# A graph layer with a mixture of experts: the gating moves from the last stage into the FFN stage

## The chip, the cores and the metric

The kernel runs on one core of a Trainium2 chip, as one launch. The metric is the device time of a launch in microseconds. A core has TensorE (PE), VectorE (DVE), ScalarE (ACT), GpSimd (POOL) and SyncE (SP), each with a queue of its own that runs in order, and 16 DMA engines that all queues share. Engines wait for each other through semaphores.

## What is computed

There are 6250 nodes of 256 features and 206,250 edges. A graph attention layer comes first; it is the same in both kernels. Then each node's row is normalised (this row is called y below), two of 16 experts are chosen for it, and their outputs, weighted by the two gates, are added to y. The sum is normalised again, scaled, shifted, and added to the node's row (x_all below).

```python
x = x + _L0_gnn_ref(_layernorm(x), edge_index, W, a_src, a_dst, gamma, beta)   # graph attention
x = x + _L0_ffn_ref(_layernorm(x)[None], gate_w, gate_b, w1, b1, w2, b2, fgamma, fbeta)[0]
...
def _L0_ffn_ref(x, gate_w, gate_b, w1, b1, w2, b2, gamma, beta):
    gate_logits = x @ gate_w + gate_b
    topk_vals, topk_idx = jax.lax.top_k(gate_logits, K)
    topk_w = jax.nn.softmax(topk_vals, axis=-1)
    h = jax.nn.relu(jnp.einsum('bsh,ehf->bsef', x, w1) + b1)
    expert_out = jnp.einsum('bsef,efh->bseh', h, w2) + b2
    sel = jnp.take_along_axis(expert_out, topk_idx[:, :, :, None], axis=2)
    moe = jnp.sum(topk_w[..., None] * sel, axis=2)
    y = x + moe
    mu = jnp.mean(y, axis=-1, keepdims=True)
    var = jnp.var(y, axis=-1, keepdims=True)
    return (y - mu) / jnp.sqrt(var + EPS) * gamma + beta
```

Everything is float32. The two gates of a node sum to 1.

## The kernel before

The 6250 nodes are 49 tiles of 128 (the last has 106). The stages run one after the other, and each ends when all its engines are done.

The graph stage (stage3) runs over the tiles. GpSimd gathers rows of source nodes with indirect DMAs, and the other engines weigh and sum them. Between this work the finishing of earlier tiles is woven in (class Finish): the inner and the outer normalisation, the choice of experts, and the lists of nodes per expert. For each tile SyncE writes y to y_rows in DRAM (keep, L1746 to L1749) and, once the tile's lists are ready, the 16 pieces of the lists (record, L1751 to L1757). ScalarE writes y of a tile into one buffer (L1708) and waits first until the last tile's y has been sent from it.

The last two tiles are finished in last_tiles. SyncE's queue holds the write of y of tile 46, the load of the first FFN bias b1T (L1789, in which each element of the transposed bias is an element of the load), and the writes of y of tiles 47 and 48. GpSimd's queue holds the loads of the first quarter of the expert weights, four iotas (L197 to L203), and six list scatters (L1673), two for each of tiles 46, 47 and 48. VectorE chooses the experts of each tile (choose, settle), which gives the scatters their places.

The list stage (stage5) makes from the lists, with a gather and a chain of small VectorE operations, the tables put_all (twice the node, plus 0 for its first choice and 1 for its second), get_all (the node) and the expert of each FFN tile.

The FFN stage (stage6) runs over some 105 tiles of 128 (node, choice) pairs, sorted by expert. It is a pipeline of steps, four to a pass of a loop. In step i TensorE transposes tile i's rows (L2090), does the first product of tile i-1 (L2099, with w1_t, a copy of the expert's weights that VectorE makes at L2132) and the second product of tile i-3 (L2108). VectorE in step i copies the weights of tile i, waits for tile i's predecessor to be transposed and writes the indices of the fetch of tile i+3 (get_at, L2124), waits for a delivery to have landed and writes the indices of the delivery of tile i-3 (put_at, L2140), waits for the second product and adds the second bias b2 (L2143, into o_sb). ScalarE copies the transposed rows (L2056), applies bias and relu (L2062), and issues the load of b2. GpSimd in step i issues the fetch of tile i+3 (L2014, a gather of rows of y_rows into xt), then the delivery of tile i-3 (L2023, a scatter of rows of o_sb into chosen). A delivery waits until the one before it has landed. SyncE loads the other quarters of the weights.

The last stage (stage7) runs over 7 groups of 7 tiles. SyncE loads both chosen rows of each node (back, L2313 to L2319) into two buffers. VectorE makes diagonal matrices of the gates (diag, L2258), ScalarE makes y again from x_all (L2204), and TensorE sums both rows, weighted, and y in PSUM (L2247 to L2249). VectorE takes the statistics of the sums (L2266 to L2271) and the scale (L2277, L2278), ScalarE normalises (L2212), and VectorE makes three passes over 7 tiles at once: times gamma (L2285), plus beta (L2286), plus x_all (L2287). GpSimd issues the outputs (L2335, L2338). In VectorE's queue group g's scale comes ahead of the sums of group g+1, and the passes of group g behind them.

## Time and profile before

| | us |
|---|---|
| median of 3 runs | 2841.47 (2836.97 to 2843.8) |
| the profiled execution, its own time | 2831.7 |
| its span in the trace | 2830.0 |

| stretch of the span, us | what runs |
|---|---|
| 0 to 2224 | the first stages and the graph stage |
| 2224 to 2264 | the last two tiles |
| 2264 to 2276 | the list stage |
| 2276 to 2700 | the FFN stage |
| 2700 to 2830 | the last stage |

Busy over the whole span: TensorE 1787.1 us (63%), VectorE 1656.7 (59%), ScalarE 1154.7 (41%), GpSimd 1839.1 (65%). Times are in microseconds from the span's start. In a timeline a row gives start, duration, engine, line, operation, what it writes and reads, and in brackets how long the engine had been idle and what released it. SPq and ACTq are DMAs issued by SyncE and ScalarE. A row with a count (x2) runs from the first start to the last end. In groups by line "busy" is the sum, then the mean of one in ns, then the idle time ahead of them with what ended it; "issue" is idle time in which nothing that the profile shows was waited for.

### The profile page before, as it was taken

To read this page: it belongs to the slowest core of one execution; us is meant where nothing else is said; L and a number is where in the kernel's file an instruction comes from. 1 tells how busy PE (TensorE), PEld (TensorE's weight loads), DVE (VectorE), ACT (ScalarE), POOL (GpSimd) and SP (SyncE) were. 2 spreads that over 40 slices of the span, in tenths; PEclk is the share of its full clock that TensorE was granted. 3 is DMA by queue.
4 is the path that set the end of the run, shared out by engine and by line. 5 is a ranking of instruction groups with operands and counts; after the bars stand their busy time and mean duration, and the time that the engine had idled before them with its cause. 6 is when DMAs were issued, how large, how long until landed. Compare 5 with 4: busy or idle time off the path is not lost. (4 is left out here: it accounts for less than half of the span.)

```text
span 2830.0 us, 43516 instructions
## 1 busy us (share of the span) xinstructions
PE 1787.1 (63%) x9175; PEld 1463.6 (52%) x9176; DVE 1656.7 (59%) x3941; ACT 1154.7 (41%) x2125; POOL 1839.1 (65%) x1939
## 2 busy tenths in 40 slices
PE   6446655655555665655655655655655379999964
PEld 4334444444444444444444544444544269999953
DVE  7646666666666666666666666666666433333356
ACT  3424434434434434434434434434434124433342
POOL 2267777777777777777777777777777335555510
PEclk9768877887778878888778787777788679999987
DMA  6444554554554554554554544544544473333353
GB/s 206 109 128 131 148 148 130 147 148 130 148 145 132 148 145 133 147 144 134 148 142 136 148 140 137 147 139 138 148 138 139 97 249 105 106 100 102 103 174 116
DMA packets 179516, 392.85 MB, mean 139 GB/s; under 512 B 52064, under 2 KB 100496, under 8 KB 173208
## 3 DMA queue, kind: packets, MB, share of 16 engines
q0 software_dynamic: 93744, 272.83, 34.1%
q1 hardware_dynamic: 69512, 105.33, 11.4%
q10 hardware_dynamic: 16224, 14.30, 2.0%
q8 instruction: 13, 0.21, 0.0%
q14 instruction: 23, 0.19, 0.0%
HBM read 355.82 MB, written 36.47 MB: 139 GB/s over the span
## 5 line engine op out<-in xcount | busy, mean ns | idle before, releaser
L1269 POOL DMA_INDIRECT gat<-table,idx x1627 | 1539.2, 946 | 506.6 <-issue 467.7
L1367 PE MATMUL ps_sum<-msg,hot 128*128 128x264 f32 x3322 | 1087.9, 498 | 804.7 <-DVE msg L1414 659.7
L1367 PEld LDWEIGHTS ps_sum<-msg,hot 128*128 128x128 f32 x3322 | 823.5, 254 | 1008.6 <-issue 819.9
L1414 DVE TENSOR_TENSOR msg<-gat,ps_weight 128x2304 f32<-128x2304 f32 x196 | 471.0, 2403 | 8.0 <-ACT ps_weight L1326 8.0
L1403 DVE TENSOR_TENSOR both<-gat,ps_own 128x144 f32<-128x144 f32 x196 | 57.8, 295 | 414.5 <-DMA gat<-table,idx 408.4
L1326 ACT ACTIVATE ps_weight<-score 128x72 f32<-128x72 f32 x196 | 45.1, 230 | 530.0 <-DVE score L1405 529.2
L1411 DVE TENSOR_TENSOR hot<-ps_own,rel 128x1152 f32<-128x1152 f32 x196 | 250.2, 1277 | 0.0
L2099 PE MATMUL ps_ht<-xT,w_t 128*128 128x128 f32 x1712 | 213.4, 278 | 1.2 <-DVE w_t L2132 0.8
L2023 POOL DMA_INDIRECT chosen<-o_sb,put_at x105 | 114.0, 1085 | 152.4 <-DMA chosen<-o_sb,put_at 73.5
L2099 PEld LDWEIGHTS ps_ht<-xT,w_t 128*128 128x128 f32 x1712 | 202.1, 194 | 5.0 <-DVE w_t L2132 3.5
L2108 PE MATMUL ps_o<-w_sb,hidT 128*128 x840 | 198.7, 379 | 0.0
L1281 ACT ACTIVATE hotT<-dst_row,neg_id 128x4352 bf16<-128x4352 int16 x48 | 187.7, 3911 | 4.9 <-PE ps_look L1353 4.9
L1283 ACT ACTIVATE hotT<-hotT 128x4352 bf16<-128x4352 bf16 x48 | 183.8, 3830 | 1.5
L2108 PEld LDWEIGHTS ps_o<-w_sb,hidT 128*128 128x128 f32 x840 | 151.6, 191 | 16.2
L2014 POOL DMA_INDIRECT xt<-y_rows,get_at x111 | 110.2, 992 | 53.1 <-issue 27.7
L1566 DVE TENSOR_TENSOR num<-acc,ps_sum 128x264 f32<-128x264 f32 x49 | 21.0, 429 | 207.8 <-PE ps_sum L1367 207.8
L2062 ACT ACTIVATE hidT<-ps_ht,b1T 128x128 f32<-128x128 f32 x424 | 120.9, 368 | 45.0 <-issue 45.0
L2056 ACT ACTIVATE xT<-ps_x 128x256 f32<-128x256 f32 x108 | 41.4, 383 | 204.8 <-PE ps_x L2090 204.8
L2132 DVE COPY w_t<-w_sb 128x1024 f32 x108 | 76.1, 705 | 78.3 <-issue 67.5
L1399 DVE TENSOR_REDUCE ps_own<-ps_look 128x144 f32<-128x432 f32 x196 | 114.3, 583 | 2.6 <-PE ps_look L1353 2.6
L1689 ACT ACTIVATE std<-var 128x1 f32<-128x1 f32 x49 | 9.9, 203 | 219.8 <-DVE var L1581 219.8
L1697 ACT ACTIVATE z<-num,nmr,rstd 128x256 f32<-128x256 f32 x49 | 29.4, 600 | 166.1 <-DVE nmr L1586 166.0
(399 smaller groups left out, 2193.2 us busy)
## 6 DMA issues: line engine op xcount, KB each, us to landing
dst_row<-dst_half SPq DMA_DIRECT2D x49, 1088.0 KB
gat<-table,idx POOLq DMA_INDIRECT x1661
b_t<-in_L_ffn_b_dram ACTq DMA_DIRECT2D x107, 128.0 KB, 3.0
w_sb<-in_L_ffn_w_dram SPq DMA_DIRECT2D x6, 2048.0 KB, 16.1
listing<-list_f SPq DMA_DIRECT2D x736, 0.5 KB
back<-chosen SPq DMA_DIRECT2D x5, 1792.0 KB, 7.7
table<-rows SPq DMA_DIRECT2D x49, 128.0 KB, 1.7
y_rows<-y SPq DMA_DIRECT2D x49, 128.0 KB, 6.0
```

Of the source, the lines that this page charges most:

```text
L1269: pool.indirect_dma_start(gat[:, GSTART[g] + k, :], None, table, bass.IndirectOffsetOnAxis(ap=idx[g][:, k:k + 1], axis=0)).then_inc(landed ...
L1281: act.activation(hotT[:, :], dst_row[:, :], ACT.Abs, bias=neg_id[:, bass.ds(t, 1)]).then_inc(apart_ready, 1)
L1283: act.activation(hotT[:, :], hotT[:, :], ACT.Relu, bias=1.0, scale=-1.0).then_inc(hotT_ready, 1)
L1367: made = pe.matmul(ps_sum[:, 0:SUM], hot[:, m, k, :], msg[:, m, k, :], start=(g == 0 and k == 0), stop=(g == NG - 1 and k == n - 1))
L1399: dve.tensor_reduce(looked[:, 0:n, :], ps_look[m][:, 0:n * SPLIT * 2 * HEADS].rearrange("p (j c h) -> p j h c", c=SPLIT, h=2 * HEADS), AX. ...
L1411: dve.tensor_tensor(hot[:, m, 0:n, :], iota.unsqueeze(1).to_broadcast([P, n, P]), rel[:, j:j + n].unsqueeze(2).to_broadcast([P, n, P]), AL ...
L1414: dve.tensor_tensor(msg[:, m, 0:n, 0:D].rearrange("p j (h d) -> p j h d", d=HD), gat[:, j:j + n, 0:D].rearrange("p j (h d) -> p j h d", d=HD),
L2014: pool.indirect_dma_start(xt[:, s, :], None, y_rows, bass.IndirectOffsetOnAxis(ap=get_at[:, s:s + 1], axis=0)).then_inc(x_in[s], 16)
L2023: pool.indirect_dma_start(chosen, bass.IndirectOffsetOnAxis(ap=put_at[:, s:s + 1], axis=0), o_sb[:, o, :], None).then_inc(o_out, 16)
L2062: last = act.activation(hidT[:, s, j * P:(j + 1) * P], ps_ht[s][:, j * P:(j + 1) * P], ACT.Relu, bias=b1T[:, bass.ds(e, 1), j:j + 1].rearr ...
L2099: last = pe.matmul(ps_ht[o][:, j * P:(j + 1) * P], w1_t[:, o, a, j * P:(j + 1) * P], xT[:, o, a * P:(a + 1) * P], start=(a == 0), stop=(a ...
L2108: last = pe.matmul(ps_o[o][:, 0:D], hidT[:, o, j * P:(j + 1) * P], w2_sb[:, bass.ds(e, 1), j, :].rearrange("p a b -> p (a b)"), start=(j = ...
```

## The change

The rows of y_rows get two columns more: the first gate and the second gate minus the first (keep_gates). SyncE writes them for each tile with a transfer of its own.

In the FFN stage VectorE turns the delivered row into what the last stage needs. With `second` (0 for a node's first choice, 1 for its second) it makes the pair's gate, and minus_y, which is -y for a first choice and 0 for a second. The delivered row is the expert's output plus b2, times the gate, minus minus_y. So the two rows of a node sum to y plus the gated outputs. The order within VectorE's step changes: weight copy, put_at, the add of b2, the gated row, then gate and minus_y of tile i-1, and then get_at. TensorE and ScalarE, which waited for o_ready, wait for o_added. In the first seven steps VectorE also adds beta to a seventh of x_all each.

The last stage has no TensorE work, no diagonals, no y and no pass for beta. VectorE adds both rows of a group in place (pair), takes statistics from there, and ScalarE normalises from there. All of `back` fits at once and is loaded in four transfers, of 1, 2, 2 and 2 groups, with no wait between them, and one for the last tile. SyncE issues the outputs too, behind the loads.

The first bias is loaded as 64 rows of 128 elements, first on SyncE's queue, transposed by TensorE ahead of the transposes of tile 47, and copied by ScalarE at its end. ScalarE's wait for it at the start of the FFN stage is gone. Some semaphores are shared, and some small tables are freed earlier.

```diff
...
-        y_rows = nc.dram_tensor("y_rows", [(TILES + 1) * P, D], F32).ap()
+        y_rows = nc.dram_tensor("y_rows", [(TILES + 1) * P, YROW], F32).ap()
...
-        dve.tensor_tensor(one(self.gates[:, bass.ds(a, 1), 1:2]), self.rsum[:, :], self.ediff[:, :], ALU.mult)
+        dve.scalar_tensor_tensor(one(self.gates[:, bass.ds(a, 1), 1:2]), self.ediff[:, :], -1.0, self.rsum[:, :],
+                                 ALU.add, ALU.mult)
...
-        sp.dma_start(self.y_rows[bass.ds(a * P, P), :], self.y[:, :]).then_inc(self.sent, 16)
+        sp.dma_start(self.y_rows[bass.ds(a * P, P), 0:D], self.y[:, :]).then_inc(self.sent, 16)
+
+    def keep_gates(self, sp, a):
+        sp.dma_start(self.y_rows[bass.ds(a * P, P), D:YROW], one(self.gates[:, bass.ds(a, 1), :])).then_inc(self.gates_out, 16)
 
     def record(self, sp, a, turn):
         self.keep(sp, a, turn)
         sp.wait_ge(self.list_ready, a + 1)
         sp.sem_inc(turn, 1)
+        self.keep_gates(sp, a)
...
+            sp.dma_start(b1_rows[:, :], b1.rearrange("e (a p) -> (e a) p", p=P)).then_inc(b1_in, 16)
             finish.keep(sp, a - 1, sp_turn)
-            sp.dma_start(b1T[:, :, :].rearrange("p e a -> p (e a)"), b1.rearrange("e (a p) -> p (e a)", p=P)).then_inc(b1_in, 16)
             finish.keep(sp, a, sp_turn)
             finish.keep(sp, b, sp_turn)
+            finish.keep_gates(sp, a - 1)
+            for n, t in enumerate((a, b)):
+                sp.wait_ge(finish.gates_ready, n + 1)
+                sp.sem_inc(sp_turn, 1)
+                finish.keep_gates(sp, t)
+            sp.wait_ge(finish.gates_out, 16 * TILES)
...
+            act.wait_ge(b1_turned, 1)
+            act.activation(b1T[:, :, :].rearrange("p e a -> p (e a)"), ps_b1[:, 0:EXPERTS * KF], ACT.Copy)
 
         @block.tensor
         def _(pe):
+            pe.wait_ge(b1_in, 16)
+            pe.transpose(ps_b1[:, 0:EXPERTS * KF], b1_rows[:, :],
+                         finish.ident[0:EXPERTS * KF, 0:EXPERTS * KF]).then_inc(b1_turned, 1)
...
+            link(dve.scalar_tensor_tensor(second[:, :], get_all[:, :], -2.0, put_all[:, :], ALU.mult, ALU.add))
...
+            sp.dma_start(bet[:, :], fbeta.unsqueeze(0).to_broadcast([P, D])).then_inc(bet_in, 16)
...
-            act.wait_ge(b1_in, 16)
...
-                        act.wait_ge(o_ready, i - 4)
+                        act.wait_ge(o_added, i - 4)
...
-                if not (head and i < 1):
-                    dve.wait_ge(x_tr, i)
-                sources((k + FFN_AHEAD) % B, i + FFN_AHEAD)
                 if not (head and i < 3):
                     if not (head and i < 5):
 
@@ -2140,7 +2173,26 @@
                     dve.tensor_copy(put_at[:, (k - 3) % B:(k - 3) % B + 1], put_all[:, bass.ds(i - 3, 1)]).then_inc(put_ready, 1)
                     dve.wait_ge(b2_in[(k - 3) % B], 16 * ((i - 3) // B + 1) if head else (i - 3 - (k - 3) % B) * (16 // B) + 16)
                     dve.wait_ge(o_done, i - 2)
-                    dve.tensor_tensor(o_sb[:, o, :], ps_o[o][:, 0:D], b2_t[:, (k - 3) % B, :], ALU.add).then_inc(o_ready, 1)
+                    dve.tensor_tensor(o_sb[:, o, :], ps_o[o][:, 0:D], b2_t[:, (k - 3) % B, :], ALU.add).then_inc(o_added, 1)
+                    dve.wait_ge(o_added, i - 2)
+                    dve.wait_ge(gate_ready, i - 2)
+                    dve.scalar_tensor_tensor(o_sb[:, o, :], o_sb[:, o, :], gate[:, (k - 3) % B:(k - 3) % B + 1],
+                                             minus_y[:, o, :], ALU.mult, ALU.subtract).then_inc(o_ready, 1)
+                if not (head and i < 1):
+                    b = (k - 1) % B
+                    dve.wait_ge(x_tr, i)
+                    if not (head and i < 3):
+                        dve.wait_ge(o_ready, i - 2)
+                    dve.scalar_tensor_tensor(gate[:, b:b + 1], xt[:, b, D + 1:YROW], second[:, bass.ds(i - 1, 1)], xt[:, b, D:D + 1],
+                                             ALU.mult, ALU.add)
+                    dve.scalar_tensor_tensor(minus_y[:, o, :], xt[:, b, 0:D], second[:, bass.ds(i - 1, 1)], xt[:, b, 0:D],
+                                             ALU.mult, ALU.subtract).then_inc(gate_ready, 1)
+                sources((k + FFN_AHEAD) % B, i + FFN_AHEAD)
+                if head and i < NGRP:
+                    if i == 0:
+                        dve.wait_ge(bet_in, 16)
+                    dve.tensor_tensor(x_all[:, i * GRP:(i + 1) * GRP, :], x_all[:, i * GRP:(i + 1) * GRP, :],
+                                      spread_tiles(bet[:, :]), ALU.add)
...
+        LOADS = ((0, 1), (1, 3), (3, 5), (5, 7))
...
+        @block.sync
+        def _(sp):
+            for n, (g0, g1) in enumerate(LOADS):
+                t0, t1 = g0 * GRP, min(g1 * GRP, FULL)
+                sp.dma_start(back[:, t0:t1, :, :].rearrange("p t c d -> p t (c d)"),
+                             chosen[2 * t0 * P:2 * t1 * P, :].rearrange("(t p c) d -> p t (c d)", p=P, c=2)
+                             ).then_inc(came[n], 16)
+                if n == 0:
+                    sp.dma_start(gam[:, :], fgamma.unsqueeze(0).to_broadcast([P, D])).then_inc(par_in, 16)
...
+            for g in range(NGRP):
+                sp.wait_ge(out_ready, g + 1)
+                t0 = g * GRP
+                nt = GRP if g < NGRP - 1 else GRP - 1
+                sp.dma_start(out[t0 * P:(t0 + nt) * P, :].rearrange("(t p) d -> p t d", p=P),
+                             normed[:, g % 2, 0:nt, :]).then_inc(out_sent[g % 2], 16)
...
-                    act.activation(normed[:, g % 2, k, :], moe(g, k), ACT.Identity,
-                                   bias=nmr_g[:, k:k + 1], scale=rstd_g[:, k:k + 1]).then_inc(norm_ready, 1)
...
-                    pe.matmul(moe(g, k), diag[:, g % 2, k, 0, :], back[:, g % 2, k, 0, :], start=True, stop=False)
-                    pe.matmul(moe(g, k), diag[:, g % 2, k, 1, :], back[:, g % 2, k, 1, :], start=False, stop=False)
-                    pe.matmul(moe(g, k), ident[:, :], y[:, g % 2, k, :], start=False, stop=True).then_inc(moe_done, 1)
...
-                dve.tensor_tensor(diag[:, g % 2, :, :, :].rearrange("p k c e -> p (k c) e"),
-                                  ident[:, :].unsqueeze(1).to_broadcast([P, 2 * GRP, P]),
-                                  gates[:, g * GRP:(g + 1) * GRP, :].rearrange("p k c -> p (k c)").unsqueeze(2).to_broadcast(
-                                      [P, 2 * GRP, P]), ALU.mult).then_inc(diag_ready, 1)
...
+            def pair(g):
+                dve.wait_ge(came[(g + 1) // 2], 32 if g >= LOADS[-1][0] else 16)
+                t0, t1 = g * GRP, min((g + 1) * GRP, FULL)
+                last = dve.tensor_tensor(back[:, t0:t1, 0, :], back[:, t0:t1, 0, :], back[:, t0:t1, 1, :], ALU.add)
+                if t1 == FULL:
+                    last = dve.tensor_tensor(back[0:LAST, FULL, 0, :], back[0:LAST, FULL, 0, :], back[0:LAST, FULL, 1, :], ALU.add)
+                link(last)
...
-                    dve.bn_stats(stats[:, k, :], moe(g, k)).then_inc(stats_read, 1)
+                    rows = P if g * GRP + k < FULL else LAST
+                    dve.bn_stats(stats[0:rows, k, :], back[0:rows, g * GRP + k, 0, :]).then_inc(stats_read, 1)
...
-                link(dve.tensor_tensor(rows, rows, spread_tiles(bet[:, :]), ALU.add))
...
```

## Rows read from the trace of the kernel before

**Rows 1.** Windows: stretch, us; busy us (x count) PE, PEld, DVE, ACT, POOL; clock, DMA, GB/s.
```profile
2700.00:2830.00 130.00, 79.23 (x294) 65.42 (x294) 81.60 (x147) 49.84 (x106) 7.21 (x8) 0.78 0.43 150
```

**Rows 2.** Timeline of the last two tiles: start, us, engine, line [idle before <-releaser].
```profile
2224.67 0.43 SPq L1789 DMA_DIRECT2D b1T<-in_L_ffn_b_dram  x1
...
2228.27 23.29 SPq L1749 DMA_DIRECT2D y_rows<-y  x2
...
2236.51 0.16 DVE L1608 SCALAR_TENSOR_TENSOR nmr<-mv,rstd 128x1 f32<-128x1 f32 x1
...
2243.36 0.95 POOL L1673 DMA_INDIRECT listing<-ids,at_i  x1 [0.30 <-issue]
2250.54 0.60 ACT L1708 ACTIVATE y<-x_all,nmr,rstd 128x256 f32<-128x256 f32 x1 [14.25 <-DMA y_rows<-y]
...
2259.72 1.55 POOL L1673 DMA_INDIRECT listing<-ids,at_i  x1 [0.30 <-issue]
...
2263.80 0.17 DVE L1900 TENSOR_SCALAR need<-taken 128x16 f32<-128x16 f32 x1 [5.56 <-PEq L1771]
```

**Rows 3.** DMA issues of the run: count, KB each, median us to landing.
```profile
xt<-y_rows,get_at POOLq DMA_INDIRECT x111, 2.8
...
b1T<-in_L_ffn_b_dram SPq DMA_DIRECT2D x1, 32.0 KB, 24.7
```

**Rows 4.** Timeline of the FFN stage, one step of its first part.
```profile
2363.54 0.99 POOL L2023 DMA_INDIRECT chosen<-o_sb,put_at  x1 [1.65 <-DVE put_at L2140]
...
2364.34 0.38 PE L2090 MATMUL ps_x<-ident,xt 128*128 128x128 f32 x2
...
2364.61 0.42 DVE L2143 TENSOR_TENSOR o_sb<-ps_o,b_t 128x256 f32<-128x256 f32 x1 [1.61 <-PE ps_o L2108]
...
2365.60 0.70 DVE L2132 COPY w_t<-w_sb 128x1024 f32 x1 [0.57 <-issue]
...
2366.52 0.15 DVE L2140 COPY put_at<-put_all 128x1 int32 x1 [0.16 <-DMA chosen<-o_sb,put_at]
...
2367.21 0.98 POOL L2023 DMA_INDIRECT chosen<-o_sb,put_at  x1 [1.42 <-DVE put_at L2140]
```

**Rows 5.** Timeline of the FFN stage, one step of its second part.
```profile
2505.10 1.22 POOL L2023 DMA_INDIRECT chosen<-o_sb,put_at  x1 [2.07 <-DMA chosen<-o_sb,put_at]
2505.50 0.69 DVE L2132 COPY w_t<-w_sb 128x1024 f32 x1 [0.56 <-issue]
...
2508.16 0.15 DVE L2140 COPY put_at<-put_all 128x1 int32 x1 [1.91 <-DMA chosen<-o_sb,put_at]
...
2509.97 0.38 PE L2090 MATMUL ps_x<-ident,xt 128*128 128x128 f32 x2
```

**Rows 6.** Timeline of the end of the FFN stage.
```profile
2687.43 0.38 PE L2090 MATMUL ps_x<-ident,xt 128*128 128x128 f32 x2
...
2697.08 0.98 POOL L2023 DMA_INDIRECT chosen<-o_sb,put_at  x1 [0.96 <-DMA chosen<-o_sb,put_at]
```

**Rows 7.** The gathers of the graph stage, one group of the page: busy, mean ns | idle.
```profile
L1269 POOL DMA_INDIRECT gat<-table,idx x1627 | 1539.2, 946 | 506.6 <-issue 467.7
```

**Rows 8.** Timeline of the graph stage, a gather beside a VectorE operation.
```profile
1535.03 0.97 POOL L1269 DMA_INDIRECT gat<-table,idx  x1 [0.30 <-issue]
1535.31 0.42 DVE L1598 SCALAR_TENSOR_TENSOR x_all<-low,x_all 128x256 f32 x1
```

**Rows 9.** Groups of the last stage: count | busy us, mean ns | idle before.
```profile
L2287 DVE TENSOR_TENSOR normed<-normed,x_all 128x1792 f32<-128x1792 f32 x7 | 14.2, 2024 | 0.2
...
L2258 DVE TENSOR_TENSOR diag<-ident,gates 128x1792 f32<-128x1792 f32 x7 | 14.0, 2017 | 6.2 <-PEq L1947 6.2
```

**Rows 10.** Loads of back<-chosen at L2316, six of them: us to landing.
```profile
DMA to landing us min/median/max: 7.6/7.7/11.4
```

**Rows 11.** Timeline of the last stage, its last group.
```profile
2816.95 2.02 DVE L2285 TENSOR_TENSOR normed<-normed,fgam 128x1792 f32<-128x1792 f32 x1 [3.42 <-ACT normed L2212]
...
2823.40 0.85 POOL L2335 DMA_DIRECT2D out_dram<-normed  x1 [8.93 <-DVE normed L2287]
```

More of the change, by code:

```diff
@@ L33 @@
 PROJ = D + 2 * HEADS
+YROW = D + 2
 GRP = 7
@@ L142, in build, with right, nsb @@
         w_in = [sem(f"w_in{q}") for q in range(4)]
-        weights, nodes = ctx.enter_context(ExitStack()), ctx.enter_context(ExitStack())
-        def right(name, shape):
-            return weights.enter_context(nc.sbuf_tensor(name, shape, F32, side="right"))
-        finish = Finish(nc, nodes, x_all, ident, rstd, nmr, gates, gw, gb, y_rows, listing)
+        weights, listers, nodes = (ctx.enter_context(ExitStack()) for _ in range(3))
+        def right(name, shape, of=weights):
+            return of.enter_context(nc.sbuf_tensor(name, shape, F32, side="right"))
+        def nsb(name, shape):
+            return nodes.enter_context(nc.sbuf_tensor(name, shape, F32))
+        mean_var = nsb("mean_var", [P, TILES, 2])
+        rstd = nsb("rstd", [P, TILES])
+        nmr = nsb("nmr", [P, TILES])
+        gates = nsb("gates", [P, TILES, 2])
+        gw = nsb("gw", [P, KD, EXPERTS])
+        gb = nsb("gb", [1, EXPERTS])
+        turn_taken = sem("turn_taken")
+        finish = Finish(nc, nodes, turn_taken, x_all, ident, rstd, nmr, gates, gw, gb, y_rows, listing)
         with ExitStack() as graph:
@@ L1478, with __init__ @@
 class Finish:
-    def __init__(self, nc, ctx, x_all, ident, rstd, nmr, gates, gw, gb, y_rows, lists):
+    def __init__(self, nc, ctx, turn_taken, x_all, ident, rstd, nmr, gates, gw, gb, y_rows, lists):
         def sb(name, shape, dt=F32):
@@ L1940, in _, with stage6 @@
             link(dve.tensor_scalar(get_all[:, :], put_all[:, :], 1, None, ALU.arith_shift_right))
-def stage6(nc, b1T, b1_in, b2, w1, w2, w1_sb, w2_sb, w_in, y_rows, chosen, ident, put_all, get_all, expert_l, passes_i):
+            link(dve.scalar_tensor_tensor(second[:, :], get_all[:, :], -2.0, put_all[:, :], ALU.mult, ALU.add))
+def stage6(nc, b1T, b2, w1, w2, w1_sb, w2_sb, w_in, y_rows, chosen, ident, put_all, get_all, second, expert_l, passes_i, turn_taken,
+           fbeta, x_all):
     with ExitStack() as ctx:
@@ L1960, in stage6 @@
         put_at = sb("put_at", [P, B], I32)
-        xt = sb("xt", [P, B, D])
+        gate = sb("gate", [P, B])
+        xt = sb("xt", [P, B, YROW])
+        minus_y = sb("minus_y", [P, 2, D])
+        bet = sb("fbet", [P, D])
         xT = sb("xT", [P, 2, D])
@@ L2151, in _, with stage7 @@
                     step(k, it * B + k, False)
-def stage7(nc, fgamma, fbeta, chosen, out, x_all, ident, rstd, nmr, gates):
+def stage7(nc, fgamma, chosen, out, x_all):
     with ExitStack() as ctx:
@@ L2211, in norm @@
                 for k in range(GRP):
-                    act.activation(normed[:, g % 2, k, :], moe(g, k), ACT.Identity,
-                                   bias=nmr_g[:, k:k + 1], scale=rstd_g[:, k:k + 1]).then_inc(norm_ready, 1)
+                    rows = P if g * GRP + k < FULL else LAST
+                    act.activation(normed[0:rows, g % 2, k, :], back[0:rows, g * GRP + k, 0, :], ACT.Identity,
+                                   bias=nmr_g[0:rows, k:k + 1], scale=rstd_g[0:rows, k:k + 1]).then_inc(norm_ready, 1)
             def root(g):
```

156 lines of the change are left out of this document (42 added, 114 removed).

## The prediction

> **What bounds the kernel now.** I read the windows first, cut at the stages, then the timeline inside each stretch that the diff touches. The graph stage fills most of the run. It is paced by GpSimd's gathers: 1627 of them, 0.946 us each, with 467.7 us of issue gaps [rows 7]. The only work that the change adds there is one 1 KB transfer per tile on SyncE's queue (the two gates), and one VectorE operation on a column takes the place of another. Neither is on GpSimd, so I cost that stage at nothing. The cover is SyncE's slack; if it were gone, SyncE would issue 47 more transfers at some 0.4 us (the 0.43 of L1789 [rows 2]), 19 us at the very most. Three stretches after it decide.
>
> *The last two tiles.* The ScalarE row of y (L1708) waits 14.25 us for `y_rows<-y` [rows 2]. VectorE had its scale ready at 2236.51+0.16. What held it: the first bias was asked for at 2224.67 in 32 KB of single elements and took 24.7 us to land, to 2249.4 [rows 2, 3]. The two writes of y behind it on SyncE's queue span 23.29 us. The next stage's first VectorE instruction starts at 2263.80.
>
> *The FFN stage.* TensorE's step starts go from 2364.34 to 2509.97 in 39 steps, 3.734 us each; from there to 2687.43 in 46 steps, 3.858 each [rows 4 to 6]. So there are two paces. In the first part a delivery (`chosen<-o_sb`) takes 0.99 us to issue and has landed when put_at starts 2.98 us later. In the second it takes 1.22 and lands after 3.06, and the weight copy (L2132, 0.69 us) lies inside its issue [rows 4, 5]. Each delivery waits for the one before: the next starts at 2367.21, 0.69 after put_at has seen the landing, so the chain runs at 3.67. Stretched by 0.2 to 0.3 it is longer than TensorE's 3.734. It then comes ahead of VectorE's copy, and that ahead of TensorE. The slow pace costs 46 x 0.124 = 5.7 us.
>
> *The last stage* is 130 us with VectorE 81.6 busy and TensorE 79.2 [rows 1]: neither is full, because they take turns (a group's sums wait for matmuls, matmuls wait for banks that VectorE and ScalarE must leave). Its end is norm, three passes of 2.02 us, and an output transfer [rows 11].
>
> **The change part by part.**
>
> *Bias in rows.* 64 rows of 512 B in place of 8192 elements, ahead of the write of y(47), with one TensorE transpose before the first tile's transposes. y(47) is issued at 2228.27 and needs to be away by 2236.7. The second tile's row y then starts at 2236.7, not 2250.54: 13.8 us earlier. What is late next: GpSimd's first four list scatters end at 2244.3 [rows 2]; the last two would start at 2244.6 and 2245.9 (13.8 before 2259.72), just behind, so the 13.8 holds. Bounds: from 14.5 (scatters no longer beside the 4-byte reads) down to 10, if the expert weights, which GpSimd asks for at the same time, hold y(47) or the bias by some us: a 128 KB gather beside a weight load is not in the rows, the median one took 2.8 [rows 3]. I take 13.8. SyncE has three small writes of gates more and must see them land. They are issued by 2244.6 and have 5 us until 2250. **-13.8.** The table of seconds is one VectorE operation on 128 columns in the list stage, under the 0.42 of 256 columns [rows 8]: **+0.3.**
>
> *FFN, steady.* VectorE now does in a step: copy, put_at, add, the gated sum, the small gate, minus_y, get_at. The two new wide ones have the form of L1598, 0.42 [rows 8], with the small one and waits 1.0 in all. Before, the add at 2364.61 is followed by the copy at 2365.60, ended 1.7 after the add [rows 4]; now it ends some 2.8 after it. TensorE wants that copy about 3.8 after the add (next step but one, after two transposes). So the cover shrinks from 2.1 to 1.0 us, and no stall remains while landings are on time. Queued behind the new place of get_at is the fetch: GpSimd waits for it before it delivers. It comes 1.5 us after the add, was 2.1 ahead of it. Fetch at 1.6 to 2.6, or to 2.9 where the copy falls in it, then the delivery at 3.2; landed 3.0 later, at 6.2, and VectorE needs it at 7.5. The fetched rows land 2.8 after issue [rows 3], at 4.4, needed at 7.2. The copy no longer lies in a delivery's issue, whichever pace the loop is in: after a landing it comes 2.3 later, the delivery is issued 0.7 to 1.7. So the slow pace has lost its cause: **-5.7.** The last delivery then starts about 3.2 after TensorE's end, 2687.43+3.9, at 2694.6, not 2697.08 [rows 6]: **-2.5.**
>
> *FFN, first seven steps.* Each adds the seventh of x_all + beta, 1792 columns, 2.02 us by L2287 [rows 9]. VectorE's loop is then 2.9+2.0 = 4.9-5.0 against 3.73. The first three steps wait for fetches and weights anyway (a row of beta comes behind weights on SyncE's queue, which falls in that time); in four the pipeline is full: 4 x 1.2 = **+4.8.** Bounds 0 and 8.
>
> *Last stage.* VectorE loses the gate diagonals (14.0) and beta (14.2) and gains the sum of both rows, 1792 columns seven times, 14.2 by the same shape [rows 9]: 81.6-14.0 = 67.6 us busy, 9.65 a group, with some 0.25 of spacing (passes are 2.05 apart for 2.02). TensorE, the kept row on ScalarE, and all waits between them are gone. But loads come larger. One of 1.8 MB alone lands in 7.7; the one issued behind 1.8 MB more lands in 11.4 [rows 10], so 1.8 MB cost some 4.6. Group 0 starts at 7.7, its sums are done at 14; groups 1 and 2 come in one load at 7.7 + 0.3 + 9.2 = 17.2. Then VectorE is never without data: 67.6-5.6+1.7 = 63.7, to 80.9; within it the last norm: 3.6 now [rows 11], 3.9 from SBUF, to 84.8. From the last pass's end (2823.1) to the span's end are 6.9; SyncE's issue saves 0.7: 91.0. **-39.0.** Bounds: -43 (no gap before group 1) and -33 (outputs queued behind the loads on the one queue hold the norms of groups 2 and 3 by up to 3 us each).
>
> **Sum:** -13.8 +0.3 -5.7 -2.5 +4.8 -39.0 = -55.9. The profiled execution took 2831.7 (span 2830.0), so its like would be 2776. It lies 9.8 below the median 2841.5. Part of that can be slow pace through the whole FFN stage, which the change would also remove; I leave that to the range. From the median: **2786**.
>
> **The rivals.**
>
> *The delivery chain keeps the pace.* VectorE's cover is halved, and each late landing now reaches TensorE. For it: the second part ran so for 46 steps. Against: its cause moves. Price: 3.858 over all of some 103 steps, 12.8 over the forecast, and no 2.5: **2801**. Chance 0.17.
>
> *VectorE's second operand holds GpSimd.* In this trace a gather that ran beside an operation with two SBUF operands took 0.97, not 0.95 [rows 7, 8]: next to nothing. A mechanism of this kernel would be: the gated sum (both operands in SBUF) falls in each delivery's issue and stretches it by its whole 0.42, chain 3.67+0.42 = 4.09, 103 x 0.36 = 37 us over: **2823**. Chance 0.05. The Trainium skill (SBUF — State Buffer, "Who interferes with whom") says that a VectorE instruction with two SBUF inputs contends with a GpSimd instruction that reads SBUF, as an exclusive lock; by it the change pays, since it adds only such instructions. For descriptor generation the page infers that it doesn't hold, and the row agrees with that.
>
> *The last two tiles give nothing back*, weights holding y as the bias did: **2800**. Chance 0.08.
>
> *The last stage is bound by its queue*, loads and outputs in one: 10 us more, **2796**. Chance 0.08.
>
> *Slower than before: the fetch comes too late.* get_at moves behind the wait for the FFN's second product, so a fetched row has 7.2-1.6 = 5.6 us to land. With a landing of L the loop over two steps is L+1.9, and beyond L = 5.6 each step costs (L-5.6)/2. It decides against the change when a step exceeds 3.734 by 55.9/103 = 0.54: L over 6.7. Rows are 1032 B, not 1024, and the median now is 2.8 [rows 3]. At L = 7.4 the time is **2786+93 = 2879**. Chance 0.03.
>
> *The matmuls weren't the cost*, VectorE's turns were; then the last stage gives only the 14.0 of busy time: **2811**. Chance 0.03.
>
> **How the numbers follow.** The forecast has 0.56, the six rivals 0.44. The low end takes the good bounds: -14.5+0.3-5.7-2.5-43 = -65, and 8 more for runs that were slow-paced throughout: 2768. The high end takes the bad ones: -10+0.3-2.5+8-33 = -37, and 6 of a graph stage not quite free, 2810; that takes in the rivals but the second, the fifth and the sixth, 0.11, and leaves as much for what I haven't seen. A change under 0.2% (5.7 us) can't be told from none. Faster 0.94, same 0.02, slower 0.04.
>
> **What would show it.** The row L1708 of the last tile should start near 2237 and the next stage near 2250. TensorE's steps should be 3.734 in both halves, except four of 4.9 at the start; a delivery should issue in 0.99 and the fetch in 1.2. The last stage should show VectorE idle once, some 3 us before the second group's sum, and 10 us a group. I am wrong if the FFN's steps exceed 3.8, if y(47) lands after 2240, or if norms wait for outputs.

## The result, and the profile after

The changed kernel takes **2811.6 us** (median of 4 runs, 2809.7 to 2816.9) where the kernel before takes 2842.6: ratio **0.990, 95% interval 0.989 to 0.992**. It is faster by some 31 us, not by 56, and its median lies 1.6 us above the range's upper end. Its profiled execution took 2810.8 (span 2809.1, before 2830.0), so the two spans differ by 20.9 where the sum said 55.9.

Cut at the stages (windows: stretch, us; busy us (x count) PE, PEld, DVE, ACT, POOL; clock, DMA share, GB/s): last two tiles, list stage, FFN stage in four pieces, last stage.

```profile
2226.40:2256.70 30.30, 5.33 (x21) 3.87 (x21) 10.69 (x59) 8.89 (x16) 9.98 (x12) 0.51 0.52 154
2256.70:2269.20 12.50, 0.85 (x2) 0.26 (x2) 5.96 (x36) 0.00 (x1) 0.99 (x1) 0.50 0.90 294
2269.20:2313.70 44.50, 31.00 (x195) 27.57 (x196) 29.07 (x56) 12.71 (x38) 22.93 (x15) 0.82 0.81 270
2313.70:2500.50 186.80, 186.80 (x1300) 174.03 (x1299) 117.99 (x350) 76.19 (x250) 101.74 (x100) 1.00 0.36 105
2504.50:2704.30 199.80, 186.12 (x1225) 164.84 (x1224) 114.58 (x332) 71.63 (x235) 108.39 (x96) 1.00 0.31 93
...
2717.00:2809.10 92.10, 0.00 (x0) 0.00 (x0) 65.61 (x141) 27.45 (x57) 0.00 (x0) 0.50 0.57 210
```

| stage | before | after | difference | forecast |
|---|---|---|---|---|
| up to the end of the graph stage | 2224.2 | 2226.4 | +2.1 | 0 |
| last two tiles | 39.5 | 30.3 | -9.2 | -13.8 |
| list stage | 12.6 | 12.5 | -0.1 | +0.3 |
| FFN: to the start of step 9 | 39.4 | 44.5 | +5.1 | +4.8 |
| FFN: steps 9 to 60 | 190.4 | 190.9 | +0.5 | 0 |
| FFN: steps 60 to 107 | 181.2 | 199.7 | +18.5 | -5.7 |
| FFN: behind the last step | 12.6 | 12.7 | +0.1 | -2.5 |
| last stage | 130.0 | 92.1 | -37.9 | -39.0 |

The large term is right. The loss sits in one row: TensorE is full in the first FFN piece (186.80 of 186.80) and loses 13.7 us in the second. Its step is 3.743 us up to step 60 and 199.7/47 = 4.25 behind it; before, the two paces were 3.734 and 3.858 [rows 4 to 6].

One step of the slow part (timeline: start, us, engine, line [idle before <-releaser]), from one delivery to the next:

```profile
2561.62 1.14 ACT L2098 ACTIVATE hidT<-ps_ht,b1T 128x128 f32<-128x128 f32 x4 [0.34 <-issue]
2562.09 0.15 DVE L2173 COPY put_at<-put_all 128x1 int32 x1 [1.14 <-DMA chosen<-o_sb,put_at]
2562.29 0.42 DVE L2176 TENSOR_TENSOR o_sb<-ps_o,b_t 128x256 f32<-128x256 f32 x1
2562.73 0.34 ACTq L2085 DMA_DIRECT2D b_t<-in_L_ffn_b_dram  x1
...
2562.76 0.98 POOL L2060 DMA_INDIRECT chosen<-o_sb,put_at  x1 [0.98 <-DMA chosen<-o_sb,put_at]
...
2563.97 0.15 DVE L2160 COPY get_at<-get_all 128x1 int32 x1
2564.60 0.69 DVE L2168 COPY w_t<-w_sb 128x1024 f32 x1 [0.49 <-issue]
...
2564.96 1.17 POOL L2051 DMA_INDIRECT xt<-y_rows,get_at  x1 [1.22 <-DVE get_at L2160]
...
2565.35 2.05 PE L2135 MATMUL ps_ht<-xT,w_t 128*128 128x128 f32 x16 [0.35 <-DVE w_t L2168]
...
2566.11 0.15 DVE L2173 COPY put_at<-put_all 128x1 int32 x1 [0.82 <-DMA chosen<-o_sb,put_at]
```

put_at starts 0.05 us after a landing, the next delivery 0.7 after it. The delivery of 2562.76 has landed at 2566.1, 3.35 later, and the next starts at 2566.80: the step is landing + 0.7. The weight copy starts 2.5 us behind the landing that put_at waited for, and TensorE waits for it. ScalarE's load of the second bias (b_t, 128 KB) goes out when hidT is done, here 0.03 us ahead of the delivery. Who waited for deliveries in this part (us, times), first in the change, 2510 to 2700, then in the kernel before, 2510 to 2680:

```profile
  DVE put_at L2173: 45.2, 45
  POOL chosen L2060: 30.2, 29
```

```profile
  DVE put_at L2140: 81.8, 44
  POOL chosen L2023: 59.8, 44
```

Both kernels hang on landings here. In both, how long one takes goes with when the b_t load is issued, counted from the delivery's start (the single rows grouped; mean time from the delivery's start to the put_at that waited for its landing, in us, and number):

| b_t load at | before | after |
|---|---|---|
| earlier than -0.5 | 2.86 (9) | 2.77 (1) |
| -0.5 to -0.2 | 3.12 (21) | 3.18 (7) |
| -0.2 to +0.05 | 3.32 (12) | 3.39 (11) |
| +0.05 to +0.3 | 3.51 (6) | 3.61 (14) |
| over +0.3 | none | 3.94 (11) |
| all | 3.17 | 3.55 |

3.17 + 0.7 and 3.55 + 0.7 are the two slow paces. In the fast part of the change the load goes out 1.5 to 1.8 us behind the delivery, and no step waits for a landing. That gave three theories. **A**: get_at, moved behind the second product's wait, makes fetch and delivery one chain. **B**: VectorE's longer step holds TensorE in any order. **C**: deliveries follow one another, and b_t loads beside them lengthen their landings.

### The profile page after: what moved, and what is told of

The parts are those of the page before. It is cut to its first block and busy times, and to the rows that moved or that the text cites. A ratio compares the mean times of both kernels' runs of the same rounds, so it can differ in the third digit from the quotient of the medians.

```text
span 2809.1 us, 43618 instructions
## 1 busy us (share of the span) xinstructions
PE 1722.8 (61%) x8882; PEld 1403.1 (50%) x8883; DVE 1770.5 (63%) x4262; ACT 1132.2 (40%) x2077; POOL 1851.3 (66%) x1931
## 5 line engine op out<-in xcount | busy, mean ns | idle before, releaser
L2051 POOL DMA_INDIRECT xt<-y_rows,get_at x111 | 131.5, 1185 | 146.3 <-DVE get_at L2160 124.2
```

The costliest lines, as they stand in the source:

```text
L2051: pool.indirect_dma_start(xt[:, s, :], None, y_rows, bass.IndirectOffsetOnAxis(ap=get_at[:, s:s + 1], axis=0)).then_inc(x_in[s], 16)
```

## The experiments

They ran on other chips, where the kernel before takes 3260 to 3270 us: the last gather of the graph stage starts at 2611 to 2647, not at 2212. The change's FFN stage (first fetch to last delivery) is 442.9 here and 442.9 and 443.9 there, and its ratio is 0.991 and 0.992, so the FFN pieces can be compared over the chips; each ratio is to the kernel before on its own chip. Paces of deliveries go from the 10th to the 53rd and from the 54th to the 104th; the 54th is late, and where the loop makes that up again they lie under TensorE's 3.734. The ratios' intervals are 0.1 to 0.3% (4 to 11 us) to each side, wider than what parts some of these edits; their trace tells them apart better.

### One part alone, and the loads taken away

*early_get*, the core of its edit:

```diff
+                if not (head and i < 5):
+                    dve.wait_ge(o_out, (i - 4) * 16)
+                if not (head and i < 1):
...
+                    dve.scalar_tensor_tensor(minus_y[:, b, :], xt[:, b, 0:D], second[:, bass.ds(i - 1, 1)], xt[:, b, 0:D],
+                                             ALU.mult, ALU.subtract).then_inc(gate_ready, 1)
+                sources((k + FFN_AHEAD) % B, i + FFN_AHEAD)
                 if not (head and i < 3):
...
-                sources((k + FFN_AHEAD) % B, i + FFN_AHEAD)
...
-                        act.wait_ge(o_added, i - 4)
+                        act.wait_ge(o_ready, i - 4)
```

> The changed kernel with VectorE's gate, minus_y and get_at of a step moved from behind the gated sum to right behind the weight copy, as the copy of get_at stood in the kernel before. minus_y gets four slots and takes the gated sum too; the sum with the second bias is made in place in b2_t, whose next load so waits for the gated sum, 0.7 us later. Theory A (the fetch behind the second product's wait makes GpSimd's fetch and delivery one chain that cannot recover): the FFN stage's second part falls from 4.25 us a step to the 3.86 of the kernel before, 47 x 0.39 = 18 us less, 2793. Theory C (each delivery waits for the one before, and the loads of the second bias that go out beside a delivery lengthen its landing from 2.8 to 3.5 and more): no gain, 4.2 to 4.4 a step, 2808 to 2818. Theory B (VectorE does 1.2 us more in each step, and holds TensorE wherever the order stands): 4.1 to 4.25 a step, 2806 to 2812.

Measured: deliveries 3.715 us apart in the first part, 4.104 in the second; FFN stage 434.2, 8.7 less than the change; ratio 0.985 (0.981 to 0.988). A's 3.86 isn't reached, C's "no gain" isn't either: 3.2 of the 8.7 come in the head, the first delivery starting 20.8 behind the first fetch, not 24.0.

*before_late_get* moves the two lines of get_at behind the add, in the kernel before:

```diff
-                if not (head and i < 1):
-                    dve.wait_ge(x_tr, i)
-                sources((k + FFN_AHEAD) % B, i + FFN_AHEAD)
                 if not (head and i < 3):
...
+                if not (head and i < 1):
+                    dve.wait_ge(x_tr, i)
+                sources((k + FFN_AHEAD) % B, i + FFN_AHEAD)
```

> The kernel before with one edit: VectorE copies get_at behind the sum with the second bias, where the change has it, not ahead of put_at. Nothing else of the change. Theory A: its second FFN part goes from 3.86 to about 4.25 a step, 46 x 0.39 = 18 us more, 2860. Theory C: as the kernel before but for the later fetch, within 4 us of 2842. Theory B: the same as the kernel before, since VectorE has nothing more to do.

Measured: ratio 1.001 (1.000 to 1.003), 0.1% and not A's 0.6%. A falls as the main cause. But the windows over deliveries (stretch, us, POOL busy (x count), clock, DMA share, GB/s) show what no theory had foreseen: the first part is the slow one, 168.00/43 = 3.91 apart, and the second the fast one, 183.86/50 = 3.68.

```profile
2764.65:2932.65 168.00, 43.21 (x43) 1.00 0.35 101
2938.87:3122.73 183.86, 49.39 (x51) 1.00 0.36 105
```

*few_b2* and *before_few_b2* leave the b_t loads out behind the first four tiles:

```diff
-                    load_b2((k - 1) % B, i - 1, e)
+                    if head and i <= B:
+                        load_b2((k - 1) % B, i - 1, e)
```

> The changed kernel, but ScalarE loads the second bias for the first four tiles alone; the later tiles add those rows again, so that part of the result is left out. Theory C: with nothing beside it a delivery lands after 2.8 us, its chain is 2.8 + 0.7 = 3.5 a step, under TensorE's 3.734, so the loop recovers from the stumble near the middle: 47 x 0.5 = 24 us less, 2788, all FFN steps 3.74. Theory A: 4.2 in the second part still, 2811. Theory B: also 4.1 to 4.25.

> The kernel before with the second bias loaded for the first four tiles alone (the later tiles add those rows again). Theory C: the second part's 3.858 a step becomes 3.74, 5.5 us less, 2837. Theories A and B have no word on the loads: 3.86 a step and 2842.

Measured: few_b2 has 3.733 in the second part, an FFN stage of 418.7, 24.2 less than the change, and a ratio of 0.987 (0.984 to 0.989). So the trace has the 24 us that C forecast, and the ratio only some 0.4 to 0.6% (14 to 18 us) against the change's 0.991 and 0.992. The kernel before without them: both parts under 3.69, ratio 0.9975 (0.996 to 0.999). VectorE waits for a landing only once (few_b2, 2930 to 3100, who waited for deliveries):

```profile
  DVE put_at L2174: 0.5, 1
```

B falls too as a cause by itself: VectorE's step is as long as in the change, and the pace is TensorE's.

### The same loads at another time

Fewer loads could also help by their mere amount. *b2_landing* and *before_b2_landing* keep them all and let SyncE issue each when a delivery has landed, so always ahead of the next one:

```diff
+            with sp.Fori(2, passes) as it:
+                for k in range(B):
+                    e = expert(sp, it * B + k, 1)
+                    sp.wait_ge(o_out, (it * B + k - 4) * 16)
+                    load_b2(sp, (k - 1) % B, it * B + k - 1, e)
```

> The changed kernel, whole, with the second bias' loads after the first seven tiles taken from ScalarE's queue to SyncE's, each released by the landing of the delivery four tiles back, the same event that releases the next delivery 0.7 us later. Theory C (a load that goes out up to 1 us around a delivery's issue lengthens its landing): every load is now 0.4 to 0.7 ahead of a delivery, landing 2.8 to 3.1, the chain 3.5 to 3.8, so the FFN stage recovers from the stumble after its 52nd delivery: second part 3.75 a step, 23 us less than the change, 2788. Against: if it is the mere amount that is moved beside a delivery and not its time, the second part stays at 4.2 and the time at 2811.

> The kernel before with the same edit on its loads of the second bias. Theory C: its second part goes from 3.86 to 3.74 a step, 5.5 us less, 2837. Against: 3.86 and 2842.

Measured: 3.747 in the change's second part, FFN stage 421.0, ratio 0.986 (0.983 to 0.989); for the kernel before 3.683, FFN stage 407.6, ratio 0.995 (0.994 to 0.997). That is 11 us less in the stage than the kernel before's 418.7, where 5.5 were forecast: some 4 of them lie behind TensorE's last step. C stands, and it is not the amount of the loads. The edit changes their time and also their queue (SyncE's for ScalarE's); no run moves the queue alone, so that the time does it rests on the grouping above, where all loads are on one queue. One landing of b2_landing (2999.98 is the first of two loads in one row):

```profile
2999.98 4.28 SPq L2031 DMA_DIRECT2D b_t<-in_L_ffn_b_dram  x2
...
3000.71 1.22 POOL L2072 DMA_INDIRECT chosen<-o_sb,put_at  x1 [0.30 <-issue]
...
3003.88 0.15 DVE L2181 COPY put_at<-put_all 128x1 int32 x1 [0.77 <-DMA chosen<-o_sb,put_at]
```

Here the load is 0.73 us ahead and the landing 3.17; over 86 deliveries with the load that far ahead the mean landing is 3.0, so the chain is 3.7 and no longer sets the pace. GpSimd hardly waits for a landing any more, VectorE does, briefly (23.5 us in 41 times, 2930 to 3100).

### The head, the stage's end, the stumble

*no_beta* leaves the seven additions out. 

> The changed kernel without the seven additions of beta to x_all in the FFN stage's first steps; beta is left out of the result. By the forecast four steps of the head get 1.2 us shorter, 4.8 us less; by the trace of the change, whose first steps are 4.8, 2.7, 3.7, 4.9, 4.9, 3.8, 5.3 and 4.7 where the kernel before has 1.7, 3.9, 3.0 and then 3.73, 7 to 10 us less, 2803. The second part stays slow by theory C, 4.2 a step.

Measured: from TensorE's first transposes to step 9 it takes 32.0 us, the change 34.7 to 34.9 in its three traces. So beta costs some 2.8, neither 4.8 nor 7 to 10; the later fetches cost 1.6, since early_get takes 33.2. Ratio 0.990 (0.988 to 0.993), as the change and not the 2803 that was expected: the first part began slow. It left the slow pace after a dozen steps without a stop of GpSimd, when a load had come 0.8 and then 1.0 us behind its delivery (the 17th and 18th), and held the fast one to the 53rd.

*combo1* is b2_landing and SyncE's wait for the gates' writes moved to GpSimd ahead of the FFN stage:

```diff
-            sp.wait_ge(finish.gates_out, 16 * TILES)
+            pool.wait_ge(gates_out, 16 * TILES)
```

> The changed kernel, whole, with the loads of the second bias released by landings on SyncE's queue, and the wait for the 49 small writes of the gates moved from the end of the last tiles' stage to GpSimd ahead of its first fetch of the FFN stage, 12 us later. Theory C with the reading that the write of 8 bytes a row, issued at 2246.4 and landed only at 2255.2, holds the stage's end 3 us: 23 + 3 less than the change, 2785; if the stage end is held by GpSimd's last scatter alone, 2788.

Measured: 6.8 us from the last scatter's end to the next stage, as with the wait (6.2 to 8.3 in the eleven traces that have the stage's end as in the change); ratio 0.984 (0.982 to 0.987), within b2_landing's interval.

*scatter_first*, *gates_after*, *probe* and *pool_head8* ran once each, so only their traces are read. *scatter_first* issues the first two list scatters ahead of the weights' loads:

```diff
+            finish.scatter(pool, a - 1, 0)
             load_weights(pool, 0, w1, w2, w1_sb, w2_sb, w_in)
             list_constants(pool)
-            for n in range(3):
+            for n in range(1, 3):
```

> The changed kernel, whole, with one edit: the two list scatters of the third last tile are issued ahead of the loads of the expert weights, so that four and not six stand close together at the stage's end. The last scatter's issue ends 7.1 us before the next stage begins in the change, 2.5 in the kernel before, where four had landed long before the last two. If the scatters' landings queue on one another, the gap falls from 7.1 to about 4.5. If the small writes of the gates hold the end, it stays at 7.

Measured: the gap is 8.3, not 4.5, and the first fetch comes 79.4 us behind the last gather, where after_again has 75.5. The write of y(47) now lands late:

```profile
2671.95 0.60 ACT L1719 ACTIVATE y<-x_all,nmr,rstd 128x256 f32<-128x256 f32 x1 [2.95 <-DMA y_rows<-y]
```

*gates_after* holds the gates' three writes back until all scatters have landed (SyncE waits for `put` at 96 first), and GpSimd waits for their landing ahead of the FFN stage. 

> The changed kernel, whole, with that last edit alone. From the end of the last scatter's issue to the next stage's first instruction it has 7.1 us, the kernel before 2.5. Gates at fault: about 2.5. Scatters by themselves: about 7. The three FFN edits aren't in it, so its time says little for itself: a stage end 4.5 us earlier is 0.14%.

Measured: with no such write in flight the last scatter, issued at 2696.03, has landed only at 2705.1, 7.5 us behind its issue's end, and the next stage begins 9.8 behind it. The gates are not at fault.

```profile
2696.03 1.56 POOL L1685 DMA_INDIRECT listing<-ids,at_i  x1 [0.30 <-issue]
2705.12 0.35 SPq L1764 DMA_DIRECT2D y_rows<-gates  x1
```

*after_again*: 

> The changed kernel as it is, on the chip of the runs beside it, for comparison: 1.0% below the kernel before; its second FFN part at 4.2 a step, and the longest gap between deliveries behind the 53rd.

Measured: 0.991 (0.988 to 0.994), 4.215 in the second part, and the gap behind the 53rd delivery (5.9 us; only the one behind the first, 6.6, is longer). *probe* has 12 gathers more ahead of the stage. 

> The changed kernel, whole, with 12 more gathers of GpSimd (into a slot that is written again) ahead of the FFN stage, each waited for: some 45 us longer. All traces so far have one gap of 5.9 to 6.7 us between two deliveries, behind the 53rd, at whatever time that comes. If the number of GpSimd's transfers sets its place, the 12 bring it 6 steps forward, behind the 47th. If the loop's own turn or a semaphore's count does, it stays behind the 53rd.

*pool_head8* has GpSimd's loop begin a turn later. 

> The changed kernel, whole, with GpSimd's FFN program written out for eight steps ahead of its loop, not four, so that the loop makes one turn fewer. The longest gap between deliveries stood behind the 53rd in all traces, with 12 more transfers ahead too. If the loop's own turns set its place, it moves one turn back, behind the 57th (or vanishes). If a semaphore's or the stage's own count does, it stays behind the 53rd.

Measured, both: the gap stays behind the 53rd, 6.4 and 5.9 us wide. Neither the number of transfers nor the loop's turns set its place. In probe GpSimd stands still for 3.05 us with nothing in the profile to wait for, and there the first part is the slow one (4.233) and the second the fast one (3.752).

```profile
2991.72 1.17 POOL L2052 DMA_INDIRECT xt<-y_rows,get_at  x1 [1.21 <-DVE get_at L2166]
2995.94 0.99 POOL L2061 DMA_INDIRECT chosen<-o_sb,put_at  x1 [3.05 <-issue]
```

### A version that beats both

*combo3* is b2_landing, early_get and beta spread out (two tiles a step in the head's eight, one a step for 32 more); *combo2* has scatter_first too, *combo4* gates_after.

```diff
+                elif more:
+                    one_tile = x_all[:, bass.ds(i + 9, 1), :].rearrange("p a d -> p (a d)")
+                    dve.tensor_tensor(one_tile, one_tile, bet[:, :], ALU.add)
```

> The changed kernel, whole, with four edits: loads of the second bias released by landings; gate, minus_y and get_at right behind the weight copy; beta added to x_all two tiles a step in the head and one a step for 32 steps, where VectorE has over 0.5 us to spare, not seven tiles in each of the first seven; and the list scatter of the third last tile issued ahead of the expert weights. Theory C: against the change 23 us from the second part, 3 from the earlier fetches in the head, 3 from beta, 3 from the scatters: 32 less, 2780, 1.1% below the change and 2.1% below the kernel before. If the edits work against each other, for one by VectorE running out of time with the 0.4 us for a tile of beta, steps of 3.9 in the first part and 2790.

> The changed kernel, whole, with three edits: loads of the second bias released by landings, gate with minus_y and get_at right behind the weight copy, beta one or two tiles a step. That is the second combination without its list scatters ahead of the weights, which had put y(47)'s write behind the weights and cost 5 us. So 5 less than that: ratio to the kernel before 0.981, FFN stage (first fetch to last delivery) 411 against the change's 443. If the early scatters' 5 us were chance, 0.9825.

> As the third combination, whole, and the three small writes of gates in the last tiles' stage issued only once the six list scatters have landed, with their own landing waited for by GpSimd ahead of the FFN stage's first fetch. If those writes (8 bytes a row) are what makes the last scatter land after 8.3 us and not 3.5, the stage's end comes 4 to 5 us earlier than in the third combination: ratio 0.9795. If scatters close together are slow by themselves, both are equal.

Measured: 0.9825 (0.980 to 0.985), 0.985 (0.983 to 0.988) and 0.986 (0.984 to 0.988), which can't be told apart. All three have FFN stages of 411.0 to 411.4, 31.6 to 31.9 less than the change. So combo3 ran once more in more rounds, beside the change.

> The third combination again, whole, in more rounds and beside the change on the same chip. From the traces its FFN stage is 31.6 us shorter than the change's (411.3 against 442.9), and nothing else differs: 1.0% below the change, ratio to the kernel before 0.981. If the recovered time is given back in the graph stage or the last one, the two ratios stay within 0.5% of each other.

> The changed kernel as it is, beside it: ratio to the kernel before 0.990.

Measured: combo3 **0.982** (0.981 to 0.983), 3205.8 us; the change 0.992 (0.990 to 0.994), 3235.3. The 31.6 us of the traces come out as 29.5. The windows over combo3's deliveries, 3.69 and 3.68 apart, and under them those of the change beside it:

```profile
2747.50:2906.35 158.85, 47.85 (x44) 1.00 0.36 107
2912.67:3096.79 184.12, 55.84 (x50) 1.00 0.36 106
```

```profile
2751.54:2933.67 182.13, 47.48 (x43) 1.00 0.31 94
2940.20:3126.26 186.06, 49.88 (x51) 1.00 0.36 104
```

Here the change itself is slow first (182.13/43 = 4.24) and fast behind the gap (186.06/50 = 3.72). Its FFN stage is 443.9, as good as the 442.9 with the halves the other way round.

## Why the prediction was wrong, step by step

**The last stage** was right: 92.1 for 91.0. VectorE starts 8.3 us in, idles 4.28 ahead of the second group, then takes 9.5 a group, 65.6 busy (I had 67.6). One norm waited for an output, as the bad bound had it; it cost 1.75:

```profile
2735.55 2.03 DVE L2289 TENSOR_TENSOR back<-back 128x1792 f32<-128x1792 f32 x1 [4.28 <-DMA back<-chosen]
...
2757.92 3.55 ACT L2268 ACTIVATE normed<-back,nmr_g,rstd_g 128x256 f32<-128x256 f32 x7 [7.39 <-DMA out_dram<-normed]
```

**The FFN's steady part** is the step that failed. I read two paces and named a cause for the slow one that a single step had shown: the weight copy inside the delivery's issue [rows 5]. The copy did leave the deliveries' issue, as forecast, and half of them take 0.98; the landings got longer all the same. "The slow pace has lost its cause" should have been tested on the other rows of the same stretch: landings anywhere from 2.8 to 3.6 in it, with the issue at 0.98, 1.22 or 1.33. My own rival "the delivery chain keeps the pace" had the mechanism, but its price was taken from a landing of the kernel before. I held 3.05 + 0.7 for a constant.

What it hangs on can be counted over all steps of the slow parts. The b_t load follows hidT, hidT TensorE's first product, and that the weight copy. The copy begins 2.54 us behind the landing that releases a delivery, 1.24 in the kernel before, since the gated sum, gate, minus_y and get_at now stand ahead of it. So the load comes later behind that landing, and the pace goes with it:

| slow part of | load behind the landing | step |
|---|---|---|
| before | 4.27 | 3.86 |
| before_late_get | 4.32 | 3.92 |
| early_get | 4.86 | 4.12 |
| after | 5.00 | 4.24 |

A landing grows by 0.88 (before) to 0.98 (after) us for each us that its load comes later, by a straight line through the single rows; a longer landing also moves the next delivery away from its load. Between these two the loop settles, at 0.47 to 0.49 us of step for each us of load (0.88/1.88, 0.98/1.98): an estimate of 0.34 to 0.36 for the 0.73 above, and 0.38 measured. It does not build up: after a longer step the next load comes earlier against its delivery (correlation -0.57 after, -0.81 before). That the loads set the landing is shown by few_b2 and b2_landing; that VectorE's work between landing and copy pushes them there is read from these rows, and no run changes that work alone. -5.7 was +19.0, and with **the last delivery** (2.5, which needed the fast pace; few_b2, which has it, gains 1.8) this is 27 of the 35 us that are missing.

**The first seven steps** came out at +5.1 for +4.8, which is luck: beta is 2.8 of it, and 1.6 is the fetch behind the gated sum, which I had costed at nothing. There I took 0.1 us from get_at to the fetch. GpSimd starts it 0.9 after get_at ends:

```profile
2487.82 0.15 DVE L2160 COPY get_at<-get_all 128x1 int32 x1
...
2488.87 1.09 POOL L2051 DMA_INDIRECT xt<-y_rows,get_at  x1 [1.35 <-DVE get_at L2160]
```

**The last two tiles**: the bias in rows did what was forecast. The second tile's y row starts at 2238.78, held by VectorE alone, where I had 2236.7 from the kernel before, and the graph stage ended 2.1 later:

```profile
2238.78 0.60 ACT L1719 ACTIVATE y<-x_all,nmr,rstd 128x256 f32<-128x256 f32 x1 [0.29 <-DVE nmr L1617]
...
2248.00 1.55 POOL L1684 DMA_INDIRECT listing<-ids,at_i  x1 [0.30 <-issue]
...
2256.74 0.17 DVE L1929 TENSOR_SCALAR need<-taken 128x16 f32<-128x16 f32 x1 [10.35 <-PEq L1786]
```

It is behind this that 4.6 us are missing. The last scatter ends at 2249.55 and the next stage begins at 2256.70, 7.1 later, 2.5 before. I had moved the stage's end with the scatters' starts ("just behind") and so kept the 2.5. The last scatter landed 8.3 us behind its issue's start, with five others in the 7.2 us ahead of it. The row was there in the kernel before: its six landed after

```profile
DMA to landing us min/median/max: 3.5/7.0/8.5
```

the last two, which stood alone [rows 2], after 3.5 and 3.6, the four in a row after 5.9, 8.1, 8.2 and 8.5. gates_after rules the gates out; scatter_first had four together and gained nothing, as these four say. Whether the scatters hold one another or something else holds them stays open: in scatter_first even the two ahead of the weights landed after 6.1 and 8.6.

**The second operand.** The rival with 0.05 came in part. In the fast part the gated sum, both operands in SBUF, begins 0.07 to 0.16 us behind a delivery's start and the issue stays at 0.98; in the slow part it begins 0.12 to 0.14 ahead in half of the steps, and the issue takes 1.20 to 1.22. That is 0.24, not 0.42; it is rather minus_y that does it (see the last section), and the landings don't follow it: in the 14 rows from 2540 to 2600 those of 1.2 land after 3.1 to 3.8, those of 0.98 after 3.4 to 4.0.

**The range** had no term for the slow pace getting slower, and its "8 for runs slow-paced throughout" had only the good sign. The sign (0.94 for faster) was right.

## What to carry to other kernels

A latency that sits in a loop is not a constant: before an edit near it is costed, group all its occurrences by what else is in flight, since a mean of 3.5 us can be a spread of 2.8 to 4.2 with one main cause. Where transfers must follow one another, tie the other loads of the step to the landing that releases them, not to an engine that drifts; here it took 22 us off the stage in the trace for a few lines. And a stage that ends with a wait for a transfer ends with its landing: read that from rows with as many neighbours in flight as the change will leave.

## What the runs showed of the hardware

A GpSimd issue that finds a weight copy running on VectorE ends 0.83 or 0.84 us behind the copy's end (87 of the 88 such fetches of the change's trace; the other 0.88), so it takes up to 1.45. One that starts first is not free of it: where the copy begins 0.18 to 0.53 us into a delivery's issue, the issue ends 0.11 to 0.13 behind the copy's end, in 39 of 39 deliveries of the kernel before, as in [rows 5] (2505.50 + 0.69, and 2505.10 + 1.22). In the 14 where the copy begins at 0.70 or later the issue keeps its 0.98 or 0.99. In these rows of the change the same 0.12 makes 0.96, which is also the undisturbed length of a fetch:

```profile
2492.60 0.96 POOL L2051 DMA_INDIRECT xt<-y_rows,get_at  x1 [1.36 <-DVE get_at L2160]
2492.74 0.69 DVE L2168 COPY w_t<-w_sb 128x1024 f32 x1 [1.04 <-issue]
```

The Trainium skill (SBUF — State Buffer, "Who interferes with whom") says of a VectorE instruction in a 2-port mode that whoever issues first holds the shared ports for the whole instruction. The first case fits that; the second doesn't, since there GpSimd's issue came first and still waited, and the copy kept its 0.69 (the trace doesn't tell the copy's mode). The page also infers that a tensor_tensor of two SBUF inputs doesn't disturb descriptor generation. For minus_y, a scalar_tensor_tensor with two, the rows speak against it: where it begins 0.68 to 0.71 us into a delivery's issue, the issue ends 0.03 to 0.05 behind its end (26 of 27), and where it begins at 0.79 or later the issue takes 0.98 to 1.00 (63 of 63):

```profile
2571.07 1.21 POOL L2060 DMA_INDIRECT chosen<-o_sb,put_at  x1 [1.03 <-DMA chosen<-o_sb,put_at]
...
2571.75 0.48 DVE L2188 SCALAR_TENSOR_TENSOR minus_y<-xt,second 128x256 f32<-128x256 f32 x1
```

The gated sum runs at the start of the same issues, so that it has no part in it is not shown.

A 128 KB scatter from GpSimd lands in 2.8 to 4.2 us, by whether a 128 KB load is issued 0.5 us ahead of it or 0.6 behind. The Trainium skill (DMA: Bandwidth & Descriptors, "Latency and other measured facts") says that a transfer's fixed cost is mostly the memory's answer, and grows with the load on the memory; that fits, though no run here separates the two.

The loop has two phases, 3.74 and 4.2 us, in one and the same kernel. Both can hold for over 40 steps, and a disturbance of a few us can tip it from either into the other; in no_beta it left the slow one without such a disturbance. The disturbance comes by itself: in all 20 traces, of both kernels and every experiment, the 54th delivery starts 5.9 to 6.7 us behind the 53rd, at 2494 to 2990 us of the run. Its cause is open.
